# Two streams on every engine: the top-k search of one item woven at a fixed share beside the layers of the next

## The chip, the cores and the metric

One Trainium2 chip, one of its cores; one launch computes the whole batch. The metric is device time in microseconds (us), the median of a few executions. The engines of a core are TensorE (PE, its weight load shown as PEld), VectorE (DVE), ScalarE (ACT), GpSimd (POOL) and SyncE (SP, here only transfers). Each has its own instruction stream and runs it in order; streams meet at semaphores alone. All data are float32 unless said otherwise.

## The reference, cut

Eight items of 512 tokens x 128 channels go through four layers, each `x = x + s(norm(x)) * silu(g(norm(x)))`. The items share nothing.

```python
# L0: s = gated delta rule, 16 heads of 8; state 8x8 per head, element by element
state = state * (1 - beta * kk) + beta * (v[:, None] * k[None]);  out_t = state @ q_t
#     g = "coupling": a chain of small dense layers with gelu, run 3 times
for _ in range(3):
    tf = sigmoid(gelu(gelu(gelu(out @ w1 + b1) @ w2 + b2) @ w3 + b3) @ w4 + b4)
    out = out + (0.1 + adaptive_range * (0.7 * gf + 0.3 * tf - 0.5) * 2) * twist(out)
# L1: s = 2 time-mix layers (state = 0.95 * state + 0.05 * k * v, a scan over tokens)
#     g = 2 x [qkv projection, l2norm, rotary, attention in windows of 64 with the one before (8 heads of 64),
#              output projection, a * gelu(g) feed-forward]
# L2: s = selective state space, 256 channels x 16 states
h = exp(dt * A_n) * h + (dt * u) * B_n[t]      # 16 scans over 512 tokens for each half of the channels
y += h * C_n[t]
#     g = mixture of 4 experts, top 2: (silu(x @ w1) * (x @ w3)) @ w2
# L3: g = the coupling again;  s = attention of 16 heads of 8 over 512 tokens, with a search
scores = q @ k.T / sqrt(8);  aw = softmax(scores)
kth = top_k(aw, 25)[-1]      # 512 // 20 = 25, for each of 16 * 512 rows
o_s = (aw * (aw >= kth), divided by its sum) @ v;  o_l = linear attention
s = (a * o_s + (1 - a) * o_l) @ Wproj
```

## The kernel before

Activations lie with the 128 channels on partitions and the 512 tokens along the free axis, so a tile is 128x512. Everything of an item stays on chip. `nc.Fori(0, B)` runs eight times over one body, and the body is four blocks one after the other, L0, `layer1()`, `layer2()`, `layer3()`. A block writes out the stream of each engine; it ends with `S.clear()`, which clears the block's semaphores and holds all engines at a barrier. Inside a block, work that does not depend on each other is written side by side by hand, and the order in the code is the order on the engine. The eight PSUM banks all belong to the block that runs; most values alternate between two banks, so that one is written while the other is read. `keep_clock` lets TensorE compute products of the identity that nobody reads, where it would stand idle.

**L0.** Eight scans of the delta rule (one for each column of the state) go beside the coupling `cp`, a chain of hops: a matmul, a pass of ScalarE, the next matmul.

**L1.** For each of two depths: the projections of q and k with their norms and rotary beside the time-mix layer (128 channels at a time), then eight units of attention (one per block of 128 queries and half of the heads), then the feed-forward. For a unit, VectorE takes the row maxima (`centre`, L828 and L832), ScalarE four exponentials with row sums (`exponent`, L721), VectorE inverts the sums (`share`, L842), GpSimd divides (L904), TensorE transposes the probabilities into two banks, and these are copied back to SBUF, the first by ScalarE (L737), the second by VectorE (`turn_probs`, L850); then come the products with v.

**L2.** After a prelude (normalisation, convolution, router, dt) a loop over n = 0..15 runs state n of the state space beside expert chunk n of the mixture (16 chunks, their weights always in SBUF). For state n VectorE computes `db` (128x1024, L1190) and then two scans (`scan`, L1170), both of whose tiles, `da` and `db`, lie in SBUF; GpSimd multiplies by C (L1220).

**L3.** After its prelude (qkv, norms) comes the search over 64 tiles of 128 query rows x 512 keys, in pairs. Per tile: TensorE computes scores, ScalarE copies them to SBUF (`fetch`) and takes the exponentials (`exponent`, L1439), and VectorE finds the 25th largest of each row by four times `max` (the eight largest) with three times `match_replace` between them (L1603, L1608, L1612): seven operations of 128x512 a tile, fourteen a pair, nearly all that VectorE does there. GpSimd compares with the 25th value and multiplies (L1662, L1669), TensorE transposes, ScalarE copies back, TensorE multiplies with v. Beside the search the code weaves the coupling of L3, the linear attention, and the opening of the next item (`Opening`: first norm, q, k, v and beta of L0). So the search of an item runs beside about 40 steps of short work; the rest of the layers, L0 to L2, has VectorE to itself.

## Time and profile before

| | |
|---|---|
| runs | 5724.26, 5734.3 (median), 5734.64 us |
| profiled execution | 5721.85 us, span 5720.0 us |
| TensorE clock granted, mean | 0.896 |
| first item starts | 69.8 us into the span |
| one item | 706.4 us |
| of the first item: L0 / L1 / L2 / L3 end at | 125.9 / 309.2 / 444.2 / 769.1 us |
| busy over the span: PE, DVE, ACT, POOL | 74%, 75%, 52%, 44% |

The profile is one execution on the core. Its span is cut into 40 slices for a first look; the views named further down cut it by stretch (windows), by instruction (timeline) or by kind of instruction (groups). "Granted clock" is the share of the full TensorE clock that the chip gave. The eight items repeat each other; the stretches shown are those of the first item, and a whole one is shown beside them.

### The profile page before, as it was taken

The page shows a single profiled execution, that of the slowest core. Times are in us where ns is not written, and L with a number is a line of the kernel's source. Part 1 is how long each engine was busy: PE and PEld are TensorE (multiplying, and loading weights), DVE is VectorE, ACT ScalarE, POOL GpSimd, SP SyncE. Part 2 cuts the span into 40 slices and gives each one's busy share as a digit, 9 for nine tenths or more (in the row PEclk, how much of TensorE's full clock was granted, in tenths as well). Part 3 has the DMA queues.
Part 4 walks back from the last instruction along what each step waited for, and adds up shares of the span by engine and source line. Part 5 has one row for each costly group of instructions (what it writes and reads, how often), then busy time and mean ns, then how long its engine had stood idle before and what let it go on. Part 6 is the DMA issues. An engine that isn't in the chain of part 4 may idle for free. (4 is left out here: it accounts for less than half of the span.)

```text
span 5720.0 us, 61822 instructions
## 1 busy us (share of the span) xinstructions
PE 4228.7 (74%) x17108; PEld 2321.5 (41%) x17108; DVE 4273.7 (75%) x8380; ACT 2946.7 (52%) x5759; POOL 2505.1 (44%) x2236
## 2 busy tenths in 40 slices
PE   5876778767787677776777777786777867777676
PEld 2434434334343443434434344342443424434344
DVE  3478964799647995479953899548994489944899
ACT  3544645446454564545645456454554545545455
POOL 0245622446224562245622466214662156621565
PEclk9998989988899898988989978999889998889988
DMA  2000000000000000000000000000000000000000
GB/s 101 1 0 3 1 3 1 0 3 1 3 1 0 3 1 3 1 2 1 1 3 1 2 1 1 3 1 2 1 1 3 1 2 1 1 3 1 2 1 3
DMA packets 3553, 23.17 MB, mean 4 GB/s; under 512 B 336, under 2 KB 336, under 8 KB 2640
## 3 DMA queue, kind: packets, MB, share of 16 engines
q1 hardware_dynamic: 3152, 18.59, 0.8%
q8 instruction: 158, 2.59, 0.2%
q14 instruction: 243, 1.99, 0.1%
HBM read 16.23 MB, written 2.36 MB: 3 GB/s over the span
## 5 line engine op out<-in xcount | busy, mean ns | idle before, releaser
L1662 POOL TENSOR_SCALAR l_pp<-l_sc,l_m 128x512 f32<-128x512 f32 x496 | 781.8, 1576 | 642.6 <-DVE l_m L1612 618.7
L1612 DVE MAX8 l_m<-l_wk 128x8 f32<-128x512 f32 x1536 | 979.9, 679 | 0.0
L1356 PE MATMUL bank<-consts,l_pp 128*128 128x128 f32 x2048 | 396.7, 326 | 499.5 <-POOL l_pp L1669 490.0
L227 PE MATMUL bank<-l_v,l_pt 128*128 128x99 f32 x4096 | 645.6, 311 | 147.4 <-ACT l_pt L1402 131.4
L1432 ACT ACTIVATE l_sc<-bank 128x512 f32<-128x512 f32 x512 | 303.0, 594 | 743.3 <-PE bank L227 742.4
L1608 DVE MATCH_REPLACE8 l_wk<-l_m,l_wk 128x512 f32<-128x512 f32 x1024 | 683.6, 675 | 0.0
L227 PEld LDWEIGHTS bank<-l_v,l_pt 128*128 128x128 f32 x4096 | 610.1, 228 | 177.7 <-ACT l_pt L1402 173.3
L227 PE MATMUL bank<-l_km,hold 128*128 128x512 f32 x1024 | 649.2, 724 | 42.5 <-DVE l_ol L1579 18.1
L1356 PEld LDWEIGHTS bank<-consts,l_pp 128*128 128x128 f32 x2048 | 280.6, 166 | 936.7 <-POOL l_pp L1669 803.8
L1669 POOL TENSOR_TENSOR l_pp<-l_pp,l_ex 128x512 f32<-128x512 f32 x496 | 630.3, 1271 | 26.7 <-ACT l_ex L1439 4.9
L1220 POOL TENSOR_TENSOR l_hc<-l_h,l_cn 128x1024 f32<-128x1024 f32 x128 | 302.4, 2362 | 674.1 <-DVE l_h L1170 674.1
L227 PE MATMUL bank<-hold,weights 128*128 128x512 f32 (+2 forms) x760 | 388.9, 645 | 86.0 <-issue 70.2
L1170 DVE TENSOR_TENSOR_SCAN l_h<-l_da,l_db 128x512 f32<-128x512 f32 x256 | 413.5, 1656 | 0.0
L1439 ACT ACTIVATE l_ex<-l_sc,l_nmx 128x512 f32<-128x512 f32 x512 | 364.4, 714 | 93.9 <-POOL l_nmx L1652 92.5
L1402 ACT ACTIVATE l_pt<-bank 128x512 f32<-128x512 f32 x512 | 301.3, 588 | 168.8 <-PE bank L1356 167.7
L904 POOL TENSOR_TENSOR l_probs<-l_probs,l_rec 128x384 f32<-128x384 f32 (+1 forms) x256 | 193.1, 773 | 373.7 <-DVE l_rec L842 373.7
L1608 DVE MATCH_REPLACE8 l_wk<-l_m,l_sc 128x512 f32<-128x512 f32 x512 | 341.8, 675 | 0.0
L1603 DVE MAX8 l_m<-l_sc 128x8 f32<-128x512 f32 x512 | 325.8, 677 | 1.4 <-ACT l_sc L1432 1.1
L895 POOL TENSOR_TENSOR l_qk<-l_of,l_t 128x512 f32<-128x512 f32 x64 | 81.0, 1266 | 513.9 <-DVE l_t L815 305.5
L227 PE MATMUL bank<-l_hc,consts 128*128 128x512 f32 x256 | 159.8, 709 | 197.1 <-POOL l_hc L1220 197.1
L1902 POOL TENSOR_TENSOR l_sq<-l_st,hold 128x512 f32<-128x512 f32 x64 | 81.0, 1266 | 508.5 <-DVE l_st L1865 508.5
L828 DVE TENSOR_REDUCE l_nmax<-bank 128x4 f32<-128x768 f32 (+1 forms) x128 | 114.1, 891 | 224.3 <-PE bank L227 214.6
(359 smaller groups left out, 8347.7 us busy)
## 6 DMA issues: line engine op xcount, KB each, us to landing
weights<-weights_dram SPq DMA_DIRECT2D x1, 11014.0 KB, 28.9
hold<-x_dram SPq DMA_DIRECT2D x9, 256.0 KB, 2.6
out_dram<-x SPq DMA_DIRECT2D x9, 256.0 KB, 3.6
consts<-consts_dram SPq DMA_DIRECT2D x1, 1503.0 KB, 32.0
rotary<-consts_dram SPq DMA_DIRECT2D x1, 1024.0 KB, 34.0
```

Source lines behind the costliest of these rows:

```text
L227: return nc.tensor.matmul(o, lhsT, rhs, start=start, stop=stop)
L1170: nc.vector.tensor_tensor_scan(hh[n % 2][:, k], da[n % 2][:, k], db[n % 2][:, k], 0.0, ALU.mult, ALU.add).then_inc(S["h"], 1)
L1220: nc.gpsimd.tensor_tensor(hc[n % 2][:], hh[n % 2][:], cn[n % 3][:, None, :].to_broadcast([128, 2, T]), ALU.mult).then_inc(S["hc"], 1)
L1356: r = nc.tensor.transpose(bank[3 + n % 2][:, 128 * k:128 * k + 128], pp[n % 2][:, 128 * k:128 * k + 128], C("ident"))
L1402: act(pt[n % 2][:], bank[3 + n % 2][:], ACT.Copy).then_inc(S["pt"], 1)
L1432: act(sc[n % RS][:], bank[n % 3][:], ACT.Copy).then_inc(S["sc"], 1)
L1439: act(ex[n % RM][:], sc[n % RS][:], ACT.Exp, scale=SC, bias=nmx[n % RM][:], accum_out=zs[:, q, h:h + 1]).then_inc(S["ex"], 1)
L1603: nc.vector.max(m8[n % RM][:, 0], sc[n % RS][:]).then_inc(S["top"], 1)
L1608: nc.vector.match_replace(w[:], m8[n % RM][:, k], sc[n % RS][:] if k == 0 else w[:], -3e38).then_inc(S["rest"], 1)
L1612: nc.vector.max(m8[n % RM][:, k + 1], wk_[n % 2][:]).then_inc(S["top"], 1)
L1662: nc.gpsimd.tensor_scalar(pp[n % 2][:], sc[n % RS][:], m8[n % RM][:, 3, 0:1], None, ALU.is_ge).then_inc(S["kept"], 1)
L1669: nc.gpsimd.tensor_tensor(pp[n % 2][:], pp[n % 2][:], ex[n % RM][:], ALU.mult).then_inc(S["pp"], 1)
```

## The change

The four blocks of an item become two streams. **Stream A** is `l0_*`, `l1_*`, `l2_*`, `l3_*`: the layers of an item up to the operands of its search (masked k, q, v, the linear attention, the gate of L3), and the opening of the next item. **Stream B** is `b_*`: the search of the item before, its products, output projection and last addition. Each is written as a Python generator per engine, and every `yield` ends a step. For each engine A has 221 steps: 25 of L0, 100 of L1 (30 hops, 22 of projections, 48 of attention: 16 units of three), 67 of L2 (9 of opening, 17 of experts, 7 hops, 32 of state loop, 2 at the end) and 29 of L3. B has 243: 3 at the start, 34 rounds of seven (32 of them with a pair of tiles; each holds the fourteen search operations, two in most steps), 2 at the end. `weave` walks A and after each of its steps lets B go on by `ROOM[kind]` steps, which is 1.1 for every kind, so that B ends with A (221 x 1.1 = 243).

`run` writes one block with the woven streams and one barrier. The program is: the opening of item 0, `run(0, True, False)` (layers alone), seven rounds of `nc.Fori(1, B)` (both), `run(B, False, True)` (search alone), a store.

With it come these edits:
- PSUM is parted. A has banks 0 to 3 and loses most of its double buffers; B has 4 and 5 for scores, 6 for transposes, 7 for products.
- SBUF is parted. B has `top` and its own tiles, A an `arena` that its layers reuse. The expert weights (3.1 MB) no longer stay; SP loads them in each round after the second attention. At the start of a round GpSimd copies four tiles from A's side to B's.
- In the attention the second copy back of a unit moves from VectorE to ScalarE (`take_turned`), and both turns of a unit use one bank.
- The experts no longer run beside the state loop but ahead of it; their silu is one pass of ScalarE, without the VectorE operation L1176.
- In the state loop and in L0 the first operand of the scans (`da`, `dec`) is written to PSUM, so the scan reads one tile from SBUF and one from PSUM.
- L0's coupling adds on GpSimd; the scaling of the rotary tables moves into other operations; a norm is no longer done in two halves; `keep_clock` is gone.
- Exponentials use one table of ScalarE, gelu and silu others: `table` puts a load wherever the woven order changes from one to another. A round of both streams has 42 loads.

```diff
+ROOM = dict.fromkeys(("hop", "l0", "pj", "at0", "at1", "at2", "wo", "ffn", "moe", "state", "states", "busy"), 1.1)
+def weave(a, b):
+    room = 0.0
+    for kind in a or ():
+        room += ROOM[kind]
+        while b is not None and room >= 1.0:
+            room -= 1.0
+            next(b, None)
+    for _ in b or ():
+        pass
...
-        bank = [banks[:, i] for i in range(8)]
+        A = [banks[:, i] for i in range(4)]
+        X, Y, P = [banks[:, 4], banks[:, 5]], banks[:, 6], banks[:, 7]
...
-        def keep_clock(b, n):
-
-            for _ in range(n):
-                mm(b[:], C("ident"), rot[:, 0])
...
+            def take_turned(i, n, e):
+                q, k = n // 2, NU * i + n
+                a.wait_ge(*S("turned", 2 * k + e + 1))
+                if k:
+                    a.wait_ge(*S("pv", k))
+                d = slice(0, 4) if q else slice(1, 4, 2)
+                act(L.pt[e][:, d], A[2].rearrange("p (s t) -> p s t", s=4)[:, d], ACT.Copy).then_inc(S["pt"], 1)
...
+                for n in range(NU):
+                    q, f, k = n // 2, n % 2, NU * i + n
+                    if n + 1 < NU:
+                        pe.wait_ge(*S("exp", 2 * k + 2))
+                        score(i, n + 1)
+                    turn(i, n, 0)
+                    yield "at0"
+                    turn(i, n, 1)
+                    yield "at1"
...
-                                nc.vector.tensor_tensor_scan(hh[n % 2][:, k], da[n % 2][:, k], db[n % 2][:, k], 0.0,
-                                                             ALU.mult, ALU.add).then_inc(S["h"], 1)
+                for k in range(2):
+                    v.wait_ge(*S("da", 2 * n + k + 1))
+                    nc.vector.tensor_tensor_scan(L.hh[n % 2][:, k], A[2 + k], L.db[:, k], 0.0, ALU.mult,
+                                                 ALU.add).then_inc(S["h"], 1)
+                yield "states"
...
+        def b_act(a):
...
+                if 1 <= p <= NP:
+                    take(p - 1, 1)
+                if p < NP:
+                    exponent(p, 0)
+                    exponent(p, 1)
+                yield
...
+        def b_dve(v):
...
+            for p in range(NP + 2):
+                for k in range(TOPK // 8 + 1):
+                    if p < NP:
+                        largest(p, 0, k)
+                        largest(p, 1, k)
+                    if k == 2 and p >= 2 and p % 8 == 1:
+                        outputs(p // 8 - 1)
+                    yield
+                    if k < TOPK // 8:
+                        if p < NP:
+                            without(p, 0, k)
+                            without(p, 1, k)
+                        yield
...
+        def run(b, item, search):
...
+                @block.vector
+                def _(v):
+                    weave(a_dve(v, first) if item else None, b_dve(v) if search else None)
...
-        with nc.Fori(0, B) as b:
+        run(0, True, False)
+        with nc.Fori(1, B) as b:
+            run(b, True, True)
+        run(B, False, True)
```

**VectorE in the attention.** In rows of the order, `l_nmax<-bank` is the row maxima of a unit and `l_rec` the inverted sums. Before:

```order
L842 RECIPROCAL l_rec<-l_zs 128x2 x2
L828 TENSOR_REDUCE l_nmax<-bank 128x4
L832 TENSOR_TENSOR l_shift<-l_nmax,l_qrs 128x4
L850 COPY l_pt<-bank 128x512
L842 RECIPROCAL l_rec<-l_zs 128x2 x2
```

After, `m<-top` (`max`) and `top<-m,top` (`match_replace`) being the search of the other item:

```order
L1189 TENSOR_REDUCE arena<-bank 128x4
L1192 TENSOR_TENSOR arena<-arena 128x4
L2045 MATCH_REPLACE top<-m,top 128x512 x2
L1201 RECIPROCAL arena<-arena 128x2 x2
L2041 MAX m<-top 128x8 x2
L2045 MATCH_REPLACE top<-m,top 128x512 x2
```

The copy is gone from VectorE; two or four operations of the search stand between the maxima and the inverted sums of a unit, and as many between one unit and the next.

**VectorE in the state loop.** The scans are listed as SCALAR_TENSOR_TENSOR; `l_hg` belongs to the experts. Before:

```order
L1190 TENSOR_TENSOR l_db<-l_du,bank 128x1024
L1170 SCALAR_TENSOR_TENSOR l_h<-l_da,l_db 128x512 x2
L1176 SCALAR_TENSOR_TENSOR hold<-hold,bank 128x512
L1181 TENSOR_TENSOR l_hg<-hold,bank 128x512
L1190 TENSOR_TENSOR l_db<-l_du,bank 128x1024
```

After:

```order
L1603 TENSOR_TENSOR arena<-arena,bank 128x1024
L2041 MAX m<-top 128x8 x2
L1610 SCALAR_TENSOR_TENSOR arena<-bank,arena 128x512 x2
L2045 MATCH_REPLACE top<-m,top 128x512 x2
L1603 TENSOR_TENSOR arena<-arena,bank 128x1024
```

The two operations of the expert have left the loop, two of the search stand behind `db` and two behind the scans, and the scans read `bank`.

**ScalarE in the experts.** L1459 is the silu of an expert's chunk, L1971 the copy of scores, L1979 the exponentials of the search, L1986 the copy back of its transposes. After:

```order
L1459 ACTIVATE arena<-bank 128x512
L1971 ACTIVATE top<-bank 128x512
L1459 ACTIVATE arena<-bank 128x512
L1986 ACTIVATE top<-bank 128x512
L316 ACT_TABLE_LOAD
L1979 ACTIVATE top,zs<-top,nmx 128x512 x2
L316 ACT_TABLE_LOAD
L1459 ACTIVATE arena<-bank 128x512 x4
```

Before, the expert's pass (L1064) stood among the exponentials of the state loop:

```order
L1073 ACTIVATE l_cn<-bank 128x512
L1077 ACTIVATE l_da<-l_dt,a_neg 128x512 x2
L1064 ACTIVATE hold<-bank 128x512
L1073 ACTIVATE l_cn<-bank 128x512
L1077 ACTIVATE l_da<-l_dt,a_neg 128x512 x2
```

Each pair of tiles of the search now brings a burst of a copy back and two exponentials to ScalarE, and in the stages that use another table a load ahead of the exponentials and one behind them.

## Rows read from the trace of the kernel before

The columns of the windows (rows 2) are: the stretch in us, its length, and then busy us of PE, PEld, DVE, ACT and POOL, each with its instructions, the granted clock, the busy share of the DMA engines, and GB/s. The stretches are, in order, L0; the boundary to L1 with L1's first norm; projections, attention and feed-forward of the first depth; the prelude of L2; its loop; the prelude of L3; its search; and a whole item.

**Rows 1.** The page: the span, and busy time of each engine.

```profile
span 5720.0 us, 61822 instructions
PE 4228.7 (74%) x17108; PEld 2321.5 (41%) x17108; DVE 4273.7 (75%) x8380; ACT 2946.7 (52%) x5759; POOL 2505.1 (44%) x2236
```

**Rows 2.** Windows: stages of the first item, last a whole item; columns are told below.

```profile
69.80:125.90 56.10, 48.30 (x96) 16.59 (x95) 30.45 (x45) 20.81 (x34) 10.12 (x8) 0.90 0.01 5
125.90:133.20 7.30, 5.14 (x10) 2.88 (x10) 3.01 (x7) 4.03 (x8) 0.00 (x0) 0.56 0.00 0
133.20:164.00 30.80, 28.96 (x98) 14.86 (x98) 18.63 (x28) 17.57 (x28) 10.62 (x8) 1.00 0.00 1
164.00:204.00 40.00, 29.92 (x260) 20.38 (x258) 14.20 (x41) 23.16 (x78) 12.07 (x16) 1.00 0.00 1
204.00:220.00 16.00, 13.06 (x33) 5.91 (x34) 6.02 (x11) 8.31 (x13) 0.00 (x0) 1.00 0.00 0
309.20:341.00 31.80, 26.53 (x70) 12.61 (x70) 15.06 (x34) 18.98 (x30) 0.00 (x0) 0.84 0.00 1
341.00:438.00 97.00, 70.20 (x177) 29.22 (x178) 91.09 (x84) 37.77 (x65) 65.16 (x31) 0.94 0.00 0
444.20:462.70 18.50, 12.41 (x32) 6.20 (x32) 11.45 (x25) 9.80 (x20) 0.43 (x1) 0.84 0.05 16
462.70:763.00 300.30, 214.35 (x965) 136.85 (x964) 293.67 (x678) 173.72 (x322) 191.84 (x191) 0.86 0.00 1
769.10:1475.50 706.40, 527.33 (x2136) 289.56 (x2136) 531.74 (x1043) 366.23 (x717) 312.75 (x279) 0.89 0.01 2
```

**Rows 3.** Timeline of VectorE in the search; columns: start, duration, engine, line, operation.

```profile
640.43 0.07 DVE L1608 MATCH_VALUE_LOAD l_wk<-l_m,l_sc 128x8 f32 x1
642.94 0.07 DVE L1608 MATCH_VALUE_LOAD l_wk<-l_m,l_wk 128x8 f32 x1
```

**Rows 4.** Timeline of TensorE and ScalarE: projections, then two hops of the coupling.

```profile
144.49 1.88 PE L227 MATMUL bank<-l_hs,weights 128*128 128x512 f32 x4
146.21 0.95 PE L227 MATMUL bank<-consts,l_of 128*128 128x2 f32 x8
...
815.39 1.07 PE L227 MATMUL bank<-L_ff,weights 128*64 128x512 f32 x2
816.50 0.68 ACT L402 ACTIVATE L_ff<-bank,weights 64x512 f32<-64x512 f32 x1 [1.17 <-PE bank L227]
817.61 1.04 PE L227 MATMUL bank<-L_ff,weights 64*32 64x512 f32 x2
```

**Rows 5.** Costliest groups of ScalarE, shapes apart.

```profile
L1439 ACT ACTIVATE l_ex<-l_sc,l_nmx 128x512 f32<-128x512 f32 x512 | 364.4, 714 | 93.9 <-POOL l_nmx L1652 92.5
L721 ACT ACTIVATE l_probs<-bank,l_shift,l_qrs 128x192 f32<-128x192 f32 x384 | 191.2, 512 | 9.5 <-DVE l_shift L832 7.0
L1439 ACT ACT_TABLE_LOAD x96 | 123.2, 1283 | 1.7
L721 ACT ACTIVATION_READ_ACCUMULATOR l_probs<-bank,l_shift,l_qrs 128x1 f32 x512 | 107.6, 210 | 0.0
```

**Rows 6.** Timeline of the last unit of an attention.

```profile
199.10 1.04 PE L525 MATMUL bank<-consts,l_probs 128*128 128x128 f32 x8
199.74 0.60 ACT L737 ACTIVATE l_pt<-bank 128x512 f32<-128x512 f32 x1 [4.80 <-PE bank L525]
```

**Rows 7.** The scans of the state loop: shortest, median, longest; then a moment of it.

```profile
L1170 DVE TENSOR_TENSOR_SCAN l_h<-l_da,l_db x256: 1192/1219/2298, 345.5 to 5376.8; 128x512 f32<-128x512 f32 x128
...
401.38 3.36 DVE L1170 TENSOR_TENSOR_SCAN l_h<-l_da,l_db 128x512 f32<-128x512 f32 x2
```

**Rows 8.** Timeline of VectorE where one item ends and the next begins.

```profile
768.43 0.69 DVE L1643 TENSOR_TENSOR x<-x,l_sc 128x512 f32<-128x512 f32 x1
775.66 0.69 DVE L426 TENSOR_REDUCE L_ctx<-hold 128x1 f32<-128x512 f32 x1 [6.55 <-issue]
```

More of the change, by code:

```diff
@@ new lines, in l0_act @@
+        def l0_act(a):
+            S, L = S0, Layer0
+            cp = L.cp.act(a)
+            a.wait_ge(*S("v", 1))
+            act(L.vv, A[1], ACT.Copy).then_inc(S["v_sb"], 1)
+            yield "hop"
+            for n in range(18):
+                i = n // 2
+                if n % 2 == 0 and i < 8:
+                    a.wait_ge(*S("pr", i + 1))
+                    act(A[0], L.pr, ACT.Identity, scale=-1.0, bias=C("one")).then_inc(S["dec"], 1)
+                next(cp)
+                yield "l0"
+            a.wait_ge(*S("gathered", 8))
+            act(L.osb, A[2], ACT.Copy).then_inc(S["osb"], 1)
+            yield "hop"
+            yield from L.norm.act(a)
+            L.cp.act_silu(a, L.cp.th)
+            yield "hop"
+            yield "hop"
```

3116 lines of the change are left out of this document (1678 added, 1438 removed).

## The prediction

> **What bounds the kernel now.** The page comes first: VectorE is busy 4274 of 5720 us and TensorE 4229, 75% and 74% [rows 1]. Neither is full, so the windows come next, one stage each [rows 2]. In the search VectorE is busy 293.67 of 300.30 us, in the loop of L2 91.09 of 97.00: those two are bound by it. Elsewhere it has room: 30.45 of 56.10 us in L0, 18.63 of 30.80 in the projections, 14.20 of 40.00 in the attention, 6.02 of 16.00 in the feed-forward. There a chain of hops sets the pace, or TensorE (28.96 of 30.80 in the projections). An item takes 706.40 us, VectorE 531.74 of them, so 174.7 us of VectorE stand empty per item: the most that any weaving can gain. 69.80 + 8 x 706.4 = 5721, the span; the profiled run took 5721.85, 12 us below the median of 5734.3.
>
> **Unit prices.** Four search operations take 642.94 - 640.43 = 2.51 us [rows 3], 0.63 each, fourteen 8.8 us. A pair has seven steps: 1.26 us of VectorE per step of B, x 1.1 = 1.39 per step of A. Two f32 matmuls of 512 columns take 146.21 - 144.49 = 1.72 us, 0.86 each, and a hop from matmul to matmul 817.61 - 815.39 = 2.2 us [rows 4]. A search exponential is 0.71 us of ScalarE, one of the attention 0.51, a row sum 0.21 behind each, a table load 1.28 [rows 5]. A copy back from PSUM is 0.60 behind a turn that ends some 0.6 after it could begin [rows 6]. A scan takes 1.22 us, but a pair was seen to take 3.36 where GpSimd worked beside it [rows 7]. A boundary between blocks costs about 775.66 - 768.43 = 7 us [rows 8].
>
> **The round of both streams, stage by stage.** For each stage there are two sums: VectorE's, which is the stage's own VectorE time plus 1.39 us per step, and that of the layers alone, which is what the chain takes now plus what the loss of double buffers adds. Where both streams meet, a hop's VectorE or ScalarE operation finds on average part of two operations of the other stream ahead of it (0.63 each, half of 1.26 us, taken as 0.5 to 0.8 per step), and the step is the chain's time plus that.
>
> - L0, 25 steps: VectorE 30.45 + 34.8, less 4 gone to GpSimd = 61; alone 25 x 2.5 = 62; woven 25 x 3.0 = **74**.
> - L1, 30 hops (first norm, ends of the attention, feed-forwards): VectorE 3.0 + 2 x 6.0 + 41.7, and what little is left = 60; alone 30 x 2.1 = 63; woven 30 x 2.6 = **78**.
> - L1, 22 steps of projections: VectorE 2 x 18.63 + 30.6 = 68; alone 62; woven **78**, since the banks are single now and both sums are near.
> - L1, attention, 48 steps: VectorE 2 x 14.20, less 10 for the copy that goes to ScalarE, + 66.7 = 85. A unit takes 40.00 / 8 = 5.0 us now, double-buffered. With one bank for both turns and the scores of the next unit behind its exponentials the loop is score 1.3, two turns 0.66 each, two copies 0.6 each, four exponentials with sums 2.9: 6.7, with waits 7.0; alone 16 x 7.0 = 112; woven 7.8 each, **124**.
> - L2, opening, 9 steps: both about 24; **27**.
> - Experts, 17 steps: VectorE 16 x 0.69 (the price of such an operation [rows 8]) + 23.6, with the four gates = 36; TensorE 16 x (3 x 0.86) with the opening of each expert, and the single bank alone 49; woven 17 x 3.7 = **63**.
> - L2, middle, 7 hops: 15 and 20; **22**.
> - State loop, 32 steps: VectorE 16 x (1.21 for `db`, twice a scan by its price, + 2 x 1.22) + 44.5 = 103. The chain alone is 62 and lies beneath: PSUM banks come free while the search runs. **106**, by the 6% and 2% that the two full stages of before stand above VectorE.
> - End of L2: **6**. L3's norm and coupling, 21 steps: VectorE 51, alone 43, woven **60**. The opening of the next item, 8 steps: 14 and 18; **22**. Boundary, once instead of four times: 7 us with twice the semaphores, **9**.
>
> The sum is T = 669 us, against 706.4. Of the 37 us gained, 19 come from the boundaries (4 x 7 less 9). The rest is small because most steps of A are hops: the search takes 1.39 us in each, and only what lies in the wait of the chain is free.
>
> **Around it.** The layers alone, no search: the sums "alone" above with 3 for the end of L2 are 518, + 9 = **527**. Search alone: the 300.30 of before [rows 2] with a start and an end = 305, + 9 = **314**. Setup and first opening: 69.80 before the first item now, **56** with fewer bytes to load and no scaling of the rotary tables (an estimate; no less than 50). Store **3**. That is 900, and 7 x 669 = 4683: span 5583, 137 below the 5720 of before. With the 2 us outside the span and the 12 by which the profiled run was quick, **5597, say 5600**. The item before ended at 5720 - 900 = 4820 = 7 x 688.6: the change pays as long as a round stays under 689 us, 20 above my sum, 0.09 us per step of A.
>
> **A rule weighed.** The pair of scans at 401.38 took 3.36 us for 2 x 1.22 [rows 7]; GpSimd was busy 65.16 of 97.00 us in that loop [rows 2]. The scans that read PSUM should lose this; my sum takes 1.22 for them. The search operations read one tile of SBUF, and no row shows them slow. The Trainium skill, "SBUF — State Buffer", section "SBUF: two separate sides", says that a VectorE operation with two SBUF inputs and a GpSimd operation lock one pair of ports, and the other waits for the whole instruction. By that rule the scans gain as I took it, and the two-tile operations of the layers, which now meet GpSimd's search work everywhere, lose; what that is worth is the third rival.
>
> **The rivals.**
> 1. *Each stage reaches the larger of its two sums.* The waits of one stream are filled exactly by the other. T = 62 + 63 + 68 + 112 + 24 + 56 (TensorE) + 20 + 103 + 3 + 51 + 18 + 9 = 589, span 900 + 4123 = 5023. For it: the search of before runs beside coupling and opening at 98% of VectorE. Against it: those were 40 steps in 300 us, spaced by hand; here there are 221 in as much search. Chance 0.20, more as a direction than to the full.
> 2. *ScalarE's bursts stand on the chain* (the slower side). Once per pair, in one step, ScalarE gets a copy back and two exponentials: 0.60 + 2 x (0.71 + 0.21) = 2.44 us [rows 5, 6]; in a gelu or silu stage two table loads more, 2.57. A hop of A behind them waits for all; the steps between have slack, but A cannot use it, being bound to its own chain. If half of a burst (1.2) counts for 32 pairs and the loads for seven, T = 669 + 38 + 18 = 725, span 5975. It decides from 20/32 = 0.6 us per pair. For it: nearly every step of A passes ScalarE. Against it: it is busy only 366 of 706 us [rows 2]. Chance 0.20.
> 3. *Ports.* Some 56 two-tile VectorE operations of A per round now run beside a GpSimd busy about half of the time (312.75 of 706.4 before, a shorter round now [rows 2]). Shortest and longest scan are 1.19 and 2.30 [rows 7], so up to 1.1 each: 56 x 1.1 x 0.48 = 29 us, T = 698, span 5786; it decides at 0.74 each. Chance 0.07 (part of it in my margin).
> 4. *The clock.* `keep_clock` is gone. Where TensorE does single hops it was granted 0.56 (the second stretch of [rows 2]), the lower level of 1.2 GHz for most of the stretch; a matmul of 0.86 us would be 1.7 there. If two thirds of the 83 hop steps of A fall low, 55 x 0.8 = 44 us: T = 713, span 5891. Against it: the search's matmuls (214 us of TensorE) now lie among the hops, at 0.86 in the search. The Trainium skill, "TensorE: Matmul & The Clock Gate", section "Part 1: The HAM clock gate", says that the low clock is the default and activity releases it; by it the denser weave would help rather than hurt. Chance 0.06.
> 5. *The streams do not overlap*, each waiting for the other: T = 518 + 305 + 9 = 832, span 6724. Chance 0.01.
>
> **Chances and range.** My forecast has 0.46. Faster than before by more than 0.2% (11 us, about what a measurement of this kernel can tell): forecast and first rival, 0.66. Within 0.2%: 0.04, from the thin place between forecast and third rival. Slower: second, fourth and fifth rival, and the rest of the third, 0.30. The range goes half of the way into the first rival and nearly to the second, 5180 to 5960; the forecast's own is 5450 to 5720.
>
> **What the profile after would show.** A round of 669 us; VectorE busy (285 for the search + 210 of layers) / 669 = 74% of it; 7.8 us from one unit of the attention to the next, 3.7 for an expert's step, 6.6 for a state; the layers alone 527, the search alone 314. Under the first rival VectorE is over 80% busy and the attention unit 7.0. Under the second, waits of TensorE and VectorE end at ScalarE, longest where table loads stand. Under the third, VectorE's two-tile operations are long beside GpSimd. Under the fourth the granted clock is below 0.8 in a round. I am wrong most easily in the time of a woven hop: 0.5 us more in each of 221 steps is 110 us a round.

## The result and the profile after

The changed kernel takes 5898.06 us (median of 4 runs, 5880.18 to 5908.12) against 5731.24 for the kernel before: a ratio of 1.0289, 95% interval 1.0262 to 1.0317. It is slower by 2.9%. The forecast was 5600 and faster; the sign was wrong, and the time lies in the range only because the range was wide (5180 to 5960). The four runs are 28 us apart, and a woven round in the profiled one takes from 705.8 to 714.1 us: where an experiment below stands on a single run, a change of 2 or 3 us in the round says nothing.

The page of the profiled execution, to be held against [rows 1]:

```profile
span 5899.2 us, 58186 instructions
PE 4249.7 (72%) x16676; PEld 1984.1 (34%) x16676; DVE 3980.5 (67%) x7874; ACT 2973.9 (50%) x5774; POOL 2541.3 (43%) x2356
PEclk8885887768876788868888678876887768877655
```

VectorE has 293 us less to do than before, and the span is 179 us longer. The clock granted to TensorE has a mean of 0.761, against 0.896.

Windows of the same trace (columns as in [rows 2]): the search alone, the round of layers alone, one round of both, and then stages. First of the round of layers alone: L0, projections, attention and feed-forward of the first depth, experts, L3 with the opening of the next item. Then of a woven round: projections, attention, experts, state loop.

```profile
5585.10:5893.40 308.30, 203.42 (x918) 97.25 (x918) 284.63 (x662) 127.82 (x271) 195.59 (x196) 0.50 0.01 2
55.80:622.00 566.20, 401.70 (x1164) 170.05 (x1164) 214.99 (x319) 232.52 (x434) 118.49 (x98) 0.75 0.02 6
1328.70:2034.50 705.80, 514.34 (x2082) 243.66 (x2082) 496.09 (x981) 371.36 (x721) 318.14 (x294) 0.79 0.02 6
...
55.80:121.00 65.20, 50.30 (x92) 16.79 (x92) 28.02 (x36) 24.42 (x35) 13.87 (x11) 0.84 0.00 1
128.20:171.10 42.90, 36.86 (x102) 17.21 (x102) 20.84 (x28) 19.00 (x30) 10.85 (x10) 0.86 0.00 1
171.10:229.90 58.80, 39.96 (x246) 24.62 (x246) 11.13 (x33) 26.35 (x84) 12.36 (x16) 0.74 0.00 1
229.90:249.20 19.30, 13.22 (x22) 4.47 (x22) 5.36 (x9) 5.93 (x9) 0.00 (x0) 0.82 0.00 0
396.80:438.20 41.40, 41.40 (x114) 19.25 (x112) 13.07 (x19) 8.97 (x15) 0.00 (x0) 1.00 0.00 1
536.70:622.00 85.30, 52.10 (x92) 18.94 (x92) 22.82 (x43) 36.87 (x54) 3.79 (x3) 0.64 0.00 0
...
1424.70:1474.40 49.70, 43.82 (x166) 21.00 (x168) 36.54 (x69) 24.70 (x44) 23.94 (x20) 0.88 0.00 0
1474.40:1542.50 68.10, 51.24 (x366) 32.59 (x362) 46.95 (x118) 41.73 (x122) 36.39 (x40) 0.82 0.00 1
1745.70:1808.00 62.30, 55.06 (x195) 26.13 (x193) 32.97 (x66) 26.17 (x43) 12.15 (x12) 0.92 0.00 1
1832.30:1934.80 102.50, 67.21 (x205) 26.00 (x205) 98.73 (x151) 47.66 (x88) 79.28 (x56) 0.58 0.00 1
```

The seven woven rounds take 709.0 us on average (from 622.0 to 5585.1). So 55.8 + 566.3 + 7 x 709.0 + 308.3 + 6 = 5899. Against the forecast: setup 56 and now 55.8; search alone 314 and 308.3; layers alone 527 and 566.3; a round 669 and 709.0. The whole miss is the 39 us in the layers alone and the 40 in each round, and these are one number: what the search adds to a round was forecast as 669 - 527 = 142, and is 709.0 - 566.3 = 142.7.

In the table below, stages are cut at operations of VectorE in each trace (an attention runs from its first row maxima to the residual sum behind it). "Before" is cut in the same way in the trace before; its L2 has experts and states in one loop, and its coupling of L3, its linear attention and its opening lie in the search.

| stage, us | before | layers alone, forecast | layers alone | woven, forecast | woven (median) |
|---|---|---|---|---|---|
| L0 with boundary | 63 | 71 | 65.2 | 83 | 87.5 |
| L1 | 183 | 237 | 250.8 | 280 | 299.4 |
| of it projections | 31.3 + 32.1 | 62 | 42.9 + 43.9 | 78 | 49.8 + 51.7 |
| of it attention | 39.8 + 39.8 | 112 | 58.8 + 55.8 | 124 | 68.1 + 67.0 |
| L2 opening | 32 (with middle) | 24 | 25.0 | 27 | 30.2 |
| experts | in the loop | 49 | 41.4 | 63 | 62.3 |
| middle | | 20 | 19.4 | 22 | 24.8 |
| state loop | 97 (with experts) | 62 | 67.3 | 106 | 103.8 |
| end of L2 | 6 | 3 | 11.8 | 6 | 12.3 |
| L3 and opening | 18.5, rest in the search | 61 | 85.4 | 82 | 91.4 |

Three groups of VectorE show what became of the ports (shortest, median, longest in ns): the scans that read PSUM, against [rows 7]; an operation with one tile in PSUM and one in SBUF; and one with both in SBUF.

```profile
L1610 DVE TENSOR_TENSOR_SCAN arena<-bank,arena x256: 1185/1199/1225, 458.8 to 5480.2; 128x512 f32<-128x512 f32 x128
...
L1226 DVE SCALAR_TENSOR_TENSOR arena<-bank,weights,rot x128: 734/742/752, 132.6 to 5157.2; 128x512 f32<-128x512 f32 x128
...
L1181 DVE SCALAR_TENSOR_TENSOR arena<-arena x64: 677/750/1687, 159.5 to 5161.5; 128x512 f32<-128x512 f32 x64
```

The longest scan is 1.23 us where it was 2.30, the operation with one tile in SBUF varies by 18 ns, and the one with two is up to 1.0 us longer than its shortest. But its whole group has a mean of 810 ns, 0.13 above its shortest: 64 x 0.13 = 8 us in the kernel, 1 us a round.

### The profile page after: what moved, and what is told of

Its sections match the earlier page's. It is cut to its first block and busy times, and to the rows that moved or that the text cites. A ratio compares the mean times of both kernels' runs of the same rounds, so it can differ in the third digit from the quotient of the medians.

```text
span 5899.2 us, 58186 instructions
## 1 busy us (share of the span) xinstructions
PE 4249.7 (72%) x16676; PEld 1984.1 (34%) x16676; DVE 3980.5 (67%) x7874; ACT 2973.9 (50%) x5774; POOL 2541.3 (43%) x2356
## 5 line engine op out<-in xcount | busy, mean ns | idle before, releaser
L2041 DVE MAX8 m<-top 128x8 f32<-128x512 f32 x2048 | 1299.9, 678 | 8.3 <-ACT top L1971 7.6
L2104 POOL TENSOR_SCALAR top<-top,m 128x512 f32<-128x512 f32 x512 | 820.0, 1602 | 1066.1 <-DVE m L2041 982.3
L2045 DVE MATCH_REPLACE8 top<-m,top 128x512 f32<-128x512 f32 x1536 | 1025.8, 675 | 0.2
L295 PE MATMUL bank<-arena,weights 128*128 128x512 f32 (+7 forms) x1200 | 685.3, 685 | 297.4 <-ACT arena L505 45.7
L295 PE MATMUL bank<-arena,consts 128*128 128x512 f32 (+1 forms) x966 | 678.1, 798 | 109.2 <-ACT arena L515 31.6
L2110 POOL TENSOR_TENSOR top<-top 128x512 f32<-128x512 f32 x512 | 649.1, 1268 | 21.1 <-ACT top L1979 3.0
L1909 PE MATMUL bank<-consts,top 128*128 128x128 f32 x2048 | 438.1, 353 | 269.4 <-POOL top L2110 252.7
L295 PE MATMUL bank<-arena 128*64 128x128 f32 (+4 forms) x3328 | 518.5, 386 | 94.5 <-ACT arena L1083 72.6
L1986 ACT ACTIVATE top<-bank 128x512 f32<-128x512 f32 x512 | 305.7, 597 | 519.4 <-PE bank L1909 519.3
L1971 ACT ACTIVATE top<-bank 128x512 f32<-128x512 f32 x512 | 302.1, 592 | 189.7 <-PE bank L295 102.1
L295 PE MATMUL bank<-kf,qm 32*128 32x512 f32 x1024 | 369.8, 800 | 8.9 <-ACT qm L1990 6.4
L1979 ACT ACTIVATE top<-top,nmx 128x512 f32<-128x512 f32 x512 | 364.9, 719 | 0.9
```

The source lines that it names most:

```text
L295: return nc.tensor.matmul(o, lhsT, rhs, start=start, stop=stop)
L1909: i = nc.tensor.transpose(Y[:, 128 * k:128 * k + 128], pp[e][:, 128 * k:128 * k + 128], C("ident"))
L1971: act(sc[slot(p, e)], X[e], ACT.Copy).then_inc(SB["sc"], 1)
L1979: act(ex[e], sc[slot(p, e)], ACT.Exp, scale=SC, bias=nmx[:, slot(p, e):slot(p, e) + 1], accum_out=zs[:, q, heads[e]:heads[e] + 1]).then_in ...
L1986: act(pt_[e], Y, ACT.Copy).then_inc(SB["pt"], 1)
L2041: nc.vector.max(m8[:, slot(p, e), k], src).then_inc(SB["top"], 1)
```

## The experiments

The length of a woven round, and in brackets that of the round of layers alone, is read from each trace as above; the changed kernel has 709.0 (566.3).

**Shares by stage.** The one rate of 1.1 becomes a list by the number of the layer step (the last step of a stage, its rate):

```diff
+SHARE = [(25, 1.1), (125, 1.3), (134, 0.8), (151, 0.5), (158, 0.8), (190, 0.4), (192, 0.8), (221, 1.72)]
-    for kind in a or ():
-        room += ROOM[kind]
+    for n, kind in enumerate(a or ()):
+        room += next(r for last, r in SHARE if n < last)
```

> Only the shares differ: search steps per layer step 1.3 in L1 (was 1.1 everywhere), 0.8 in the openings of L2, 0.5 in the experts, 0.4 in the state loop, 1.72 in L3; 243 in all as before. In the changed kernel the price of a search step, the stage in a round of both streams less the stage in the round of layers alone, is 36/35 = 1.0 us in the state loop and 20/19 = 1.1 in the experts, but 0.3 to 0.6 in L1 and nearly nothing in L3. Theory (an equal share is the wrong share; VectorE and TensorE are full in those two stages): state loop 103 to about 80, experts 61.5 to about 50, L1 up by 10, L3 up by 5 to 10; the round 708.7 to about 690, the kernel about 5765 us. Rival (a search step costs the same wherever a chain has to pass it): what two stages lose the others take back, the round stays within 5 us of 708.7.

Measured: 5856.7 us, a ratio of 1.0236 to before (1.0207 to 1.0264); round 702.8. State loop 103.8 to 81.5, experts 62.3 to 51.3, as expected; but L1 grew from 299.4 to 324.0, its two attentions from 135.1 to 151.6, for 20 search steps more. That is 1.2 us for each, a little more than the 1.0 to 1.1 that the experts and the state loop give back for each, though the steps that were there already had cost 0.3 to 0.6. The price at the margin is not the mean one. L3 took 18 steps for 4 us, and that is the gain: these shares bring 6 us a round, where 19 were expected.

**No table for the search's exponentials.** Instead of the exponential ScalarE makes a scaled copy with an offset, of the same size; the weights are then no exponentials.

```diff
-                exp_table()
-                act(ex[e], sc[slot(p, e)], ACT.Exp, scale=SC, bias=nmx[:, slot(p, e):slot(p, e) + 1],
+                act(ex[e], sc[slot(p, e)], ACT.Identity, scale=SC, bias=nmx[:, slot(p, e):slot(p, e) + 1],
```

> The exponential of the search is replaced by a copy with scale and offset of the same size (the weights of the top-k values are then not exponentials), so that it needs no table of ScalarE; the layers keep theirs. About 17 of 42 table loads of 1.28 us go from a round. If the bursts of ScalarE with their loads stand on the chain (second rival of the prediction) the round gets 15 to 22 us shorter, to 687 to 694. If they are hidden, it stays within 4 us of 708.7.

Measured: 5668.73 us in one run, round 675.3 (569.9): 33.7 us less. Groups of the changed kernel, then of this one, show the loads (out of all rounds, 120 of them gone, 17.1 a round):

```profile
L316 ACT ACT_TABLE_LOAD x323 | 414.4, 1283 | 129.0 <-PE bank L295 121.4 <-DVE arena L1260 3.0
```

```profile
L316 ACT ACT_TABLE_LOAD x203 | 260.4, 1283 | 128.0 <-PE bank L295 122.6 <-DVE arena L1260 3.0
```

17.1 loads are 22 us of ScalarE, and the round gained more, more also than the 15 to 22 us expected. The copy itself is no shorter (719 ns, as the exponential), so it isn't that, and the bursts of ScalarE are still there. The gain lies where loads were: experts 62.3 to 49.3, L0 87.5 to 80.9, L3 without the opening 76.5 to 70.8, the second attention 67.0 to 59.9; the state loop, where the table was in place, 103.8 and 104.4. This is the largest single price found in the woven rounds. ScalarE among the experts of the changed kernel shows how it comes about:

```profile
1746.43 0.60 ACT L1459 ACTIVATE arena<-bank 128x512 f32<-128x512 f32 x1 [0.73 <-PE bank L295]
1749.64 0.60 ACT L1986 ACTIVATE top<-bank 128x512 f32<-128x512 f32 x1 [2.61 <-PE bank L1909]
1750.26 1.28 ACT L316 ACT_TABLE_LOAD   x1
1751.55 0.72 ACT L1979 ACTIVATE top<-top,nmx 128x512 f32<-128x512 f32 x1
1752.18 0.19 ACT L1979 ACTIVATION_READ_ACCUMULATOR top<-top,nmx 128x1 f32 x1
1752.27 0.70 ACT L1979 ACTIVATE top<-top,nmx 128x512 f32<-128x512 f32 x1
1752.88 0.19 ACT L1979 ACTIVATION_READ_ACCUMULATOR top<-top,nmx 128x1 f32 x1
1753.09 1.28 ACT L316 ACT_TABLE_LOAD   x1
1754.38 0.60 ACT L1459 ACTIVATE arena<-bank 128x512 f32<-128x512 f32 x1
1757.15 0.60 ACT L1459 ACTIVATE arena<-bank 128x512 f32<-128x512 f32 x1 [2.17 <-PE bank L295]
```

Without a burst one silu (L1459) follows the other after 2.8 us (1754.38 to 1757.15). With it, they are 7.95 us apart (1746.43 to 1754.38), and TensorE has one bank for that product. Of the 5.2 us more the two loads are 2.57; the rest goes to the copy back with the wait for it and to the two exponentials.

**A product that nobody reads before each turn of the search.** It goes to the bank of the turn, behind the wait that finds this bank free and ahead of the wait for GpSimd.

```diff
-                pe.wait_ge(*SB("pp", 2 * p + e + 1))
                 if 2 * p + e:
                     pe.wait_ge(*SB("pt", 2 * p + e))
+                mm(Y[:, 0:512], C("ident"), rot[:, 0, 0:512])
+                pe.wait_ge(*SB("pp", 2 * p + e + 1))
```

> Before each turn of the search's probabilities TensorE multiplies the rotary table by the identity once (512 columns, nobody reads it), where it would wait for GpSimd: 64 such products a round, 55 us of TensorE at the high clock. If the low clock (0.79 in a round, 0.50 in the search alone, against 0.89 in an item before) is what makes the round long, the granted clock rises over 0.9 and the round falls by 15 us or more. If the clock is only a mark of a TensorE that waits anyway, the clock rises and the round stays within 5 us, or grows by what the products take. The search alone (308 us, bound by VectorE) does not change under either.

Measured: 5892.88 us in one run, round 707.1. The granted clock of the woven rounds rose from 0.78 to 0.86, not over 0.9, and the round hardly moved: attention 135.1 to 123.3, but L0 87.5 to 92.2, L3 without the opening 76.5 to 78.7, experts 62.3 to 63.8. So these products are no remedy for the whole round, though they are one for the attention. The run does not tell what the low clock by itself costs a round, since what the products cost is in the same 2 us.

**The round of layers alone, two edits.** Projections alternate between A's banks and the search's, which are free there; from the state loop on TensorE makes a product at each step.

```diff
+        def pair(n):
+            return X if alone[0] and n % 2 else A[0:2]
...
+                        for n, kind in enumerate(steps):
+                            if n >= 158 and not search:
+                                mm(Y, C("ident"), rot[:, 0])
```

> Two edits in the round of layers alone, where the search's four banks are free. The projections of L1 use them for every second step, so that they are double-buffered as before the change; and from the state loop on, TensorE makes one product of 512 columns that nobody reads at each step. The other rounds are as they were. If the loss of double buffers made the projections long, they fall from 43.4 to about 31 us each. If the low clock (0.50 to 0.62 there) made L3 and the opening long, these fall from 85.4 to 70 or below; if it is the chain of semaphores and table loads, they stay over 80.

Measured: 5868.74 us in one run; round of layers alone 545.4. Projections 42.9 and 43.9 to 40.1 and 40.4: double banks are worth 3 us each, a quarter of what they lost, where all of it was expected. L3 with the opening 85.4 to 75.8, between the two expectations. The window of that stretch:

```profile
525.10:600.90 75.80, 63.18 (x150) 25.31 (x150) 22.79 (x43) 36.75 (x54) 3.78 (x3) 0.93 0.00 0
```

TensorE does 58 instructions more in 9.5 us less, at 0.93 of its clock and not 0.64. There the low clock (0.64 in the window from 536.70, shown with the result) did cost, in a chain whose hops are single matmuls with nothing beside them. It was at the lower level of 1.2 GHz (0.50) all through the state loop before, where TensorE had 44 of 66 us of work.

**Silu of the experts from tanh.** One table serves both; VectorE has the operation again that the change had taken away.

```diff
-                    table(SILU)
-                    act(L.h1[n % 2], A[1], ACT.Silu).then_inc(S["h1"], 1)
+                    table(TANH)
+                    act(L.h1[n % 2], A[1], ACT.Tanh, scale=0.5).then_inc(S["h1"], 1)
...
+                    stt(L.h1[n % 2], L.h1[n % 2], 1.0, A[1], ALU.add, ALU.mult).then_inc(S["silu"], 1)
```

> The silu of the experts is computed from tanh, as in the kernel before: one table of ScalarE then serves the experts and the search's exponentials, so that no load is left among the 17 steps of the experts (three fewer a round), and VectorE takes one more operation of 0.66 us per chunk. With the search's exponentials off their table the experts had fallen from 62.3 to 49.3 us. If the loads did that, they fall to 52 or less here too, in spite of the 16 operations; if it was something else, they stay at 60 or more. Round: about 700 against 709.

Measured: 5857.73 us in one run, round 702.1. The experts take 52.3 us instead of 62.3, and 26 loads are gone (297 for 323): four in each woven round, 38 for 42, while the round of layers alone has two more. The woven round is 6.9 us shorter, within the expectation. This reaches the same stage by a second way, with real exponentials and 9.6 us more of VectorE in it (42.60 us busy for 32.97), and gives back 10 of the 13 us. The loads are the cause there.

**More table loads.** Where the search finds its table in place, another is loaded and then its own again.

```diff
+                if e == 0 and now[0] in (LN, TANH):
+                    table(GELU)
                 exp_table()
```

> Two table loads more, 2.57 us, ahead of every pair of exponentials of the search that finds its table in place: the suspected cost doubled. Taking away 14.7 loads a round shortened it by 33.7 us, 2.3 us for a load of 1.28. Theory (loads stand on the chain of both streams, and what waits behind them adds to it): the round grows by 50 us or more, most in the attention; the state loop (VectorE full) and the search alone by little. Rival (the exponential without a table gained in some other way, loads are mostly hidden): the round grows by less than 20 us.

Measured: 6217.24 us in one run; loads 679 for 323, of them 62 in the search alone, so 42 more a round; round 750.8, 41.8 us more, less than the 50 expected. A load costs 1.0 us of a round here, less than the 2.0 of the loads taken away. Of the 42, 17 stand in the two attentions, which take 16 us more (151 for 135), and 10 in the state loop, which takes 6 more. In the search alone 62 loads cost 24 us. So the price of one depends on where it stands: 0.4 us in the search alone, 0.6 in the state loop, 0.9 in the attention, and up to 2.0 for those taken away among gelu and silu.

**Shares again**, (125, 1.1), (134, 1.0), (151, 0.8), (158, 1.0), (190, 0.75), (192, 1.0), (221, 1.74).

> Shares again, as the stages of the first try priced them: about 2 us for each search step added in L1's attention, 1.0 to 1.1 for each taken from state loop and experts, 0.3 for each added in L3. So L1 and L0 stay at 1.1, the experts have 0.8, the state loop 0.75, L3 1.74. State loop about 93, experts 57, L3 with opening 94; the round about 697 against 709 and 702.8. If price is a matter of which steps meet and not of how many, it is no better than 703.

Measured: 5877.64 us in one run, round 705.2. State loop 92.6 and experts 55.3 as expected, L3 with opening 103 where 94 was, and L0 92.7 for 87.5 with no change of its own rate. The round missed its 697 and is no better than with the first shares.

What happened to L0 shows in rounds of one and the same execution, here of the first shares, 63 to 73 us into the third woven round and into the fifth:

```profile
2089.00:2099.00 10.00, 8.40 (x34) 2.96 (x32) 3.10 (x8) 3.23 (x6) 4.34 (x6) 0.87 0.01 2
3490.90:3500.90 10.00, 10.00 (x28) 3.19 (x27) 1.51 (x5) 1.57 (x3) 3.53 (x5) 0.50 0.00 0
```

From the start of the round to the first projection of L1 the third takes 94.2 us, the fifth 100.5, with the same instructions. In the changed kernel that clock is 0.50 in one woven round (98.5 us) and 0.79 to 0.96 in the others (92.0 to 96.7); with the second shares it is 0.51 in six of the seven (100.6 to 101.1) and 0.96 in the first (91.9). So L0 is longer in the rounds whose end of L0 runs at the lower level. What decides which rounds these are, no run shows.

**Together**: these shares, tanh, products beside attention and L3, both edits of the first round.

> These shares, the experts by tanh, products of TensorE that nobody reads beside the attention and L3 alone (the attention fell from 135 to 123 us with them, L0 grew by 5), and the edits of the round of layers alone. If the parts add up: shares -12, experts -5, attention -12, L3 -5, so a round of 675 and a kernel of about 5640 us, faster than before the change by 1.5%. If the gains overlap, as parts of one chain do, the round is 685 to 695 and the kernel about 5720 to 5790.

Measured: 5771.28 us, 1.007 of before (1.0046 to 1.0093), round 693.9 (549.5). Of the 34 us that the parts promised, 15 came. That need not be overlap: the shares alone brought 4 of their 12 (round 705.2); tanh alone brought 7; the attention stands at 130 and not at 123; and L0 is some 5 us longer in four of the seven rounds, with the clock of its end at 0.53.

**Not woven.** The search begins and then waits until the layers are through.

```diff
+SHARE = [(1, 1.0), (221, 0.0)]
```

> The shares are one step at first and then nothing, so that in each round the layers run alone and the search after them: the same instructions, not woven. If the two sums are what they look like (layers alone 566.3 us, search alone 308.3), a round takes about 566 + 300 = 866 us, and the weaving hides 157 us of the search in a round of 709; an item before, 706.4 us, hid it less but had layers that were shorter by about 160 us. Kernel about 7000 us. If the layers are slowed by the second stream's mere presence (its start, the copies, the banks), the round is over 880.

Measured: 7055.2 us in one run, round 873.9 (566.4): the layers 573, the search behind them 300.7. The weaving hides 873.9 - 709.0 = 165 us of the search, 55% of it. That is a net gain, for the two kernels differ in more than order: with the search by itself its exponentials need one load in all, and this kernel has 204 loads for 323, 25 a round for 42. The 17 loads a round are put in by the weaving itself.

**Banks of the attention in the round of layers alone**, with the projections as above: scores on two pairs, the two turns of a unit on a bank each.

```diff
+        def both(k):
+            return banks[:, 4:6] if alone[0] and k % 2 else banks[:, 0:2]
+        def turned_in(e):
+            return Y if alone[0] and e else A[2]
```

> Only in the round of layers alone: projections on two pairs of banks, and in the attention scores on two pairs of banks and the two turns of a unit on a bank each, as before the change. The attention took 39.8 us a depth before (first row maxima to the first residual sum), 58.8 and 55.8 in this round. If the loss of banks is the reason, it falls to 42 to 46 us a depth. If the copy that moved from VectorE to ScalarE, or the order of the steps, is, it stays over 52.

Measured: 5861.58 us in one run, round of layers alone 535.7. The attention falls from 58.8 and 55.8 to 45.9 and 46.0, with the copies still on ScalarE. Windows of the first depth, before the change and in this kernel:

```profile
164.20:204.00 39.80, 29.72 (x258) 20.27 (x256) 14.20 (x41) 23.16 (x78) 12.07 (x16) 1.00 0.00 1
```

```profile
166.00:211.90 45.90, 35.85 (x248) 22.03 (x246) 11.00 (x32) 26.12 (x84) 12.36 (x16) 0.81 0.00 1
```

Banks account for 23 of the 35 us that the attention had lost. Of what is left, one thing shows in the rows: the clock is 0.81 and not 1.00, and TensorE is busy 6 us longer for fewer matmuls. The next kernel has the same attention in its round of layers alone, and there the first depth happened to run at 0.96:

```profile
169.50:211.00 41.50, 30.63 (x246) 19.13 (x244) 10.87 (x33) 26.23 (x84) 12.36 (x16) 0.96 0.00 1
```

41.5 us, 1.7 above the kernel before: the rest of the loss in this depth is the clock, and what is left for the moved copy and the order of the steps is at most 2 us. In the projections it is the same. With the banks doubled, their second depth took 42.0 us at 0.88 (this run), 40.4 at 0.92 (the kernel of the two edits) and 38.7 at 0.96 (the kernel below without tables for the search).

**The combination, with these banks and products beside the end of L0.**

> The combination before this one (round 694), with products that nobody reads also beside the end of L0, where its clock fell and the stage took 92.6 instead of 87.5 us, and with the banks of the attention in the round of layers alone. Round about 688, round of layers alone about 525; kernel about 5710 us, within 0.5% of the kernel before the change. If the end of L0 is not a matter of the clock, the round stays at 694 and the kernel at about 5750.

Measured: 5723.27 us (10 runs), 1.0003 of before, 0.9990 to 1.0017; round 691.4 (519.2). The end of L0 did not move (93.2 for 92.6). But the products did not raise the clock there either: 63 to 73 us into a round it is 0.53 in six of the seven, so the run does not test whether it is a matter of the clock. The kernel is as fast as before the change.

**The same without tables for the search.**

> The same with the search's exponentials replaced by copies with scale and offset, so that no table load comes with them (the weights of the top-k values are then not exponentials). It tells whether the loads still stand on the chain once shares and clock are better: with 17 loads a round at 1.5 to 2 us each it is 25 to 34 us a round less than the kernel beside it, about 660, kernel about 5510 us; if the gains overlap, less than 15 us a round.

Measured: 5588.13 us in one run, round 670.7: 20.7 us less for 15.1 loads a round, 1.4 us each, between the two expectations. With 5588 us against 5720 for the kernel before, the loads stand between the corrected weave and a gain of 2.3%. This is a bound and not a kernel, since its weights are no exponentials.

**One bank of the search for the second turn, in every round.**

```diff
-                for e, g in enumerate(groups):
-                    i = mm(X[e], qm[32 * g:32 * g + 32, r, 128 * q:128 * q + 128], kf[32 * g:32 * g + 32])
-                i.then_inc(SB["score"], 1)
+                g = groups[e]
+                mm(X[0], qm[32 * g:32 * g + 32, r, 128 * q:128 * q + 128], kf[32 * g:32 * g + 32]).then_inc(SB["score"], 1)
...
-                        r = nc.tensor.transpose(A[2][:, 128 * (2 * s + d):128 * (2 * s + d) + 128],
+                        r = nc.tensor.transpose([A[2], X[1]][e][:, 128 * (2 * s + d):128 * (2 * s + d) + 128],
```

> The search's two tiles of a pair take turns on one bank for their scores, and the bank that is set free holds the second turn of each unit of the attention, in every round. The search pays with matmuls that no longer run side by side, some 20 us of TensorE a round. In the round of layers alone a bank for each turn and pair of scores took 22.7 us from the attention. If the bank of the turn matters beside the search too, the attention of a woven round falls from 135 to 125 us or less, the round by 5 to 10 us; if there the wait is for ScalarE and VectorE, it stays within 3 us of 135, and the round grows by what the scores cost.

Measured: 6111.52 us in one run, round 735.2 (549.6), search alone 352.8. In the round of layers alone this one bank is worth 18 us (47.8 and 48.4 for 58.8 and 55.8), most of what all of them were. In a woven round the attention is 137.2, as it was. The search pays more than the 20 us of TensorE expected, 50 us for each item; the group of its scores, in the page of the changed kernel and then in the groups of this one:

```profile
L295 PE MATMUL bank<-kf,qm 32*128 32x512 f32 x1024 | 369.8, 800 | 8.9 <-ACT qm L1990 6.4
```

```profile
L295 PE MATMUL bank<-kf,qm 32*128 32x512 f32 x1024 | 771.2, 841 | 115.4 <-ACT top L1973 108.8 <-ACT qm L1992 6.3
```

TensorE's time for them doubles, and TensorE waits for the copy between them. That is (771.2 - 369.8) / 256 pairs = 1.6 us a pair, and the two attentions of a woven round hold 7.5 pairs: 12 us more of TensorE in them, and they grew by 2. So the bank may be worth up to 10 us there, or nothing, if TensorE's extra time was covered. What banks cost beside the search stays open.

> The same beside the best combination (round 691.4, attention 125.6, kernel 5723 us). If the bank matters, attention 115, round 683, kernel about 5665 us, 1% faster than the kernel before the change; if it does not, round 690 to 695 and no difference from it that can be measured.

Measured: 6146.65 us, 1.0742 of before (1.0727 to 1.0757), round 742.6 (519.2). The attention is 146.8 for 125.6, L3 without the opening 103 for 90. The same edit costs 51 us a round here and cost 26 before; that a fuller TensorE is the reason was not tested.

## Why the prediction was wrong

**What the search adds to a round** was forecast as 142 us and is 142.7. But the reason given was incomplete: 34 of the 143 are the table loads that the search brings, which the sum had left to the second rival. That rival had the right mechanism and the parts wrong: it took 7 pairs of loads for 18 us, and 17 loads cost 34; its 38 us for the bursts themselves were measured by no run, since the bursts stayed where the loads were taken out. If the loads are 34, what the sum reckoned for waits in front of VectorE (0.5 to 0.8 us a step) was too much by as much. That two errors met is luck, and the agreement of 142 with 142.7 proves nothing for the sum.

**The layers alone: the step that failed.** The sum had 527 us, the trace 566.3, and the same 39 us are missing from each woven round. For several stages it took times of the kernel before, though they had lost their second banks and the high clock.
- *Projections, "alone 62"*: 86.8. The text said that banks are single now and yet took the time of before for the layers alone. Two pairs of banks bring back 3 us a depth. The clock is another part (0.86 in that stretch, before 1.00): from 0.88 to 0.96 it gave 3.3 us of a depth. Where the rest, 5 to 7 us a depth, comes from was not settled; the trace shows a tail of four copies of v ahead of the first scores, where before the scores began behind two.
- *Attention*: 112 forecast, 114.6 measured; the loop reckoned from its durations held, and of the 35 us more than before 23 are the banks.
- *L3, norm, coupling and opening, "alone 43 + 18"*: 85.4. Ten are the clock. A hop was priced at the 2.2 us of a chain at full clock ([rows 4]), and the products that raised the clock from 0.64 to 0.93 took 9.6 us off the stretch. Of the 25 loads of this round 8 stand here, 10 us of ScalarE, since the own exponentials of L3 stand between the gelus of the coupling; how much of them the chain feels was not measured.
- *End of L2, 3*: 11.8. Behind the last scan come GpSimd's product, four operations of VectorE, four matmuls (3.78 us) and two more operations, one behind the other; they were booked as an end of the loop.
- *Hops of L1, 63*: too dear by some 14, which covered part of the above. *Experts, 49*: 41.4, with TensorE busy all the time.

**Why it is slower than before** follows from the same rows. Before, an item was 706.4 us; the stages outside the search and its tail took 393 of them, and the search hid coupling, linear attention and opening in its 300. The layers alone of the changed kernel take 566.3: 67 more in L1 (250.8 for 183.3), 67 in L3 (85.4 for 18.5) for coupling and opening that used to lie beside the search, 30 in L2 (164.9 for 135.0) whose experts had lain beside the states, 9 in L0. The weaving hides 165 us of the search (some 199 if the 17 loads that it puts in, 34 us, are left out), and the layers grew by 173 to make it possible; the search with its ends is 308 us for 313. A round of 709.0 is an item of 706.4 again. On top comes what a pipeline of two stages costs at its ends: nine rounds for eight items, 55.8 + 566.3 + 308.3 + 6 = 936 us around seven rounds, where 776 (69.8 and one item) stood around seven items, + 160. 7 x 2.6 + 160 = 178 of the 179 us. The forecast had those ends as 900, so it saw them. Break-even was really 683 us a round.

**The rivals.** *Larger of two sums* (589 us): nowhere near. *Ports*: the gain was right, 413.5 - 297.4 = 116 us of scans in all, 14.5 an item; the loss is 1 us a round in the largest group and not 29. The Trainium skill, "SBUF — State Buffer", section "SBUF: two separate sides", says that an operation of VectorE with two SBUF inputs takes a pair of ports that it shares with GpSimd. The trace agrees: the scans, with one input in SBUF now, take 1.19 to 1.23 us with GpSimd busy 79.28 of 102.50 us beside them, and so do the two other groups shown with the result. The price in the rival was wrong because it let each such operation lose 1.1 us in 0.48 of the cases; the median one of the group shown took 0.07 us more than the shortest. *The clock*: it fell as the rival said, 0.761 over the kernel. In the layers alone products that nobody reads took 10 us off L3, and an attention took 41.5 us at 0.96 for 45.9 at 0.81. In the woven rounds such products took 12 us off the attentions but 2 off the round, at a clock of 0.86. Whether the low clock costs the rival's 44 us there stays open, because no run had a high clock without paying for it; 6 us lay between two L0 of one execution, one with its end at 0.87 and one at 0.50. *No overlap* (832 us): measured as an experiment, 873.9.

The range was said to go half of the way into the first rival; 5180 is nearly three quarters of it (5583 to 5023). Chances of 0.66 for faster were too high for one reason above all: the forecast stood 20 us from break-even on a sum over twelve stages, and for the chains at single banks and at the low clock it used durations of a kernel that had neither.

## What to carry to other kernels

Before two streams are woven, put a price on what the weave takes from each of them alone: banks, double buffers, and the work that already lay side by side. If a stream grows by as much as the other one is hidden, nothing is won, and the ends of the pipeline are lost. Give each stage its own share, count for each engine and not for VectorE alone, and look for the table of ScalarE at every place where the streams meet: here a load of 1.28 us cost from 0.4 to 2.0, and a silu made of tanh, which lives in the table in place, was worth 9.6 us more of VectorE.

## What the runs showed of the hardware

- Scores of two row groups into two banks ran side by side on TensorE (800 ns each, 1024 of them in 369.8 us busy); sent to one bank with a wait between, the same 1024 instructions took 771.2 us.
- A table load of 1.28 us cost 0.4 us in the search alone, 1.0 where it was added in woven rounds, 1.4 to 2.0 where it was taken away among gelu and silu.
- The same attention, instruction for instruction, took 41.5 us at a granted clock of 0.96 and 45.9 at 0.81.
- Woven rounds with the same instructions differ: 705.8 to 714.1 us in the changed kernel, 703.1 to 710.0 with the products that nobody reads. Part of it lies at the end of L0, where the granted clock was near 0.50 in some rounds and above 0.79 in others of one execution; with the first shares that went with 6 us of L0 (100.5 for 94.2).
